# A two-layer transformer block on one core: a round's MLP parts dealt out anew over its steps, and a later start of GpSimd on the second layer's weights

## The reference

```python
def layer0(x, t):                    # 16 heads of 32, 4 key/value heads, sparse mask
    scale, shift = split(t @ W_ada.T + b_ada)
    h = layernorm(x) * (1 + scale) + shift
    q = rope(h @ Wq.T); c = h @ Wkd.T          # latent of 128
    k = rope(c @ Wku.T); v = c @ Wvu.T
    p = softmax(mask(q @ k.T / sqrt(32)))      # window 64, every 64th key, no future block
    return x + (p @ v) @ Wo.T

def layer1(x, pos, t):               # 8 heads of 64, one key/value head, no mask
    h = rms(x) * ln1_w * (1 + t @ ln1_tw.T)
    q, k, v = rope(h @ Wq.T), rope(h @ Wk.T), h @ Wv.T
    x = x + (softmax(q @ k.T / 8) @ v) @ Wo.T
    h = rms(x) * ln2_w * (1 + t @ ln2_tw.T)
    return x + (silu(h @ Wg.T) * (h @ Wu.T)) @ Wd.T    # inner width 2048
```

## Time and profile before

| | us |
|---|---|
| median of three runs | 1840.02 |
| lowest and highest | 1840.02, 1841.26 |
| the profiled execution | 1837.08 |
| its span, first to last instruction | 1835.2 |
| first pair's attention, alone | about 206.7 |
| first round | 214.0 |
| six rounds that follow, together | 1281.3 |
| last pair's MLP, alone | 133.2 |

### The profile page before, as it was taken

The page is one execution under the profiler, slowest core; times in us unless marked ns, Lnnn a source line. Parts: engine busy times, 40 slices in busy tenths (PEclk is TensorE's granted clock), DMA queues, the critical chain, the costliest instruction groups (busy, mean ns, idle before and its releaser), DMA issues.

```text
span 1835.2 us, 38092 instructions
## 1 busy us (share of the span) xinstructions
PE 1716.1 (94%) x12416; PEld 931.6 (51%) x12416; DVE 1161.6 (63%) x2956; ACT 945.7 (52%) x2775; POOL 400.3 (22%) x554
## 2 busy tenths in 40 slices
PE   6576898999999999999999999999999999999999
PEld 2244444555455545555455554555455554555444
DVE  6869566574667558684576756675586855766320
ACT  3836456364664538554483546645385544835320
POOL 6038586011111111111110111111111111101120
PEclk9777999999999999999999999999999999999999
DMA  7876489462784439653593627844395626936220
GB/s 238 142 189 113 125 198 233 100 122 72 169 162 100 81 107 195 129 116 77 130 191 88 115 75 171 158 102 79 108 195 128 118 74 136 187 90 110 98 69 23
DMA packets 527259, 234.56 MB, mean 128 GB/s; under 512 B 476336, under 2 KB 493744, under 8 KB 527024
## 3 DMA queue, kind: packets, MB, share of 16 engines
q1 hardware_dynamic: 527024, 231.72, 57.8%
HBM read 90.09 MB, written 16.78 MB: 58 GB/s over the span
## 4 chain that ended last, share of the span: by engine, by line
PE 74%; DVE 9%; DMA 9%; ACT 3%; issue 3%; SPq 1%; POOL 0%; DVEq 0%; ACTq 0%; POOLq 0%
PE up L1390 8%; PE gate L1390 8%; PE gate L1392 8%; PE gate L1391 8%; PE up L1392 7%; PE up L1391 7%; DMA prob_t<-prob 7%; PE bank L1390 4%; PE bank L1392 4%; PE bank L1391 4%; PE y L1390 4%; PE y L1392 4%; PE y L1391 4%; PE bank L1417 2%; DVE prob L1081 2%
## 5 line engine op out<-in xcount | busy, mean ns | idle before, releaser
L851 ACT ACTIVATE bank<-bank,low 128x128 f32<-128x128 f32 (+2 forms) x768 | 302.0, 394 | 74.5 <-DVE low L1074 46.8
L695 POOL TENSOR_TENSOR inner_t<-inner,inner_t 128x512 f16<-128x512 f32 x128 | 148.8, 1162 | 671.8 <-ACT inner_t L1019 671.8
L1081 DVE TENSOR_TENSOR prob<-bank,prob 128x512 f16<-128x512 f32 (+1 forms) x320 | 202.7, 634 | 47.1 <-ACT prob L860 45.7
L860 ACT ACTIVATE prob<-bank 128x512 f16<-128x512 f32 (+1 forms) x320 | 178.4, 557 | 56.2 <-DMA prob_t<-prob 33.6
L1345 DVE SCALAR_TENSOR_TENSOR silu<-silu,gate 128x512 f32<-128x512 f32 x128 | 87.9, 686 | 187.1 <-ACT silu L1013 186.0
L1390 PE MATMUL up<-mlp,ring 128*128 128x512 f16 x512 | 195.1, 381 | 5.7 <-DVE inner L1355 5.6
L1390 PE MATMUL gate<-mlp,ring 128*128 128x512 f16 x512 | 194.4, 380 | 0.9 <-DVE mlp L1050 0.9
L1391 PE MATMUL up<-mlp,ring 128*128 128x512 f16 x512 | 195.1, 381 | 0.0
L1392 PE MATMUL up<-mlp,ring 128*128 128x512 f16 x512 | 195.0, 381 | 0.0
L1392 PE MATMUL gate<-mlp,ring 128*128 128x512 f16 x512 | 194.5, 380 | 0.0
L1391 PE MATMUL gate<-mlp,ring 128*128 128x512 f16 x512 | 194.5, 380 | 0.0
(11 more groups left out here) (176 smaller groups left out, 4034.7 us busy)
## 6 DMA issues: line engine op xcount, KB each, us to landing
ring<-wgu_dram SPq DMA_DIRECT2D x112, 512.0 KB, 4.0
x_in<-x_dram SPq DMA_DIRECT2D x18, 512.0 KB, 5.0
x_res<-x_mid SPq DMA_DIRECT2D x16, 512.0 KB, 3.5
wgu_dram<-ring SPq DMA_DIRECT2D x16, 512.0 KB, 3.5
out_dram<-x_res SPq DMA_DIRECT2D x32, 256.0 KB, 2.3
prob_t<-prob SPq DMA_TRANSPOSE x256, 3.5
inner_t<-wd_t_dram SPq DMA_DIRECT2D x4, 1024.0 KB, 8.7
ring<-wg_t_dram SPq DMA_DIRECT2D x16, 256.0 KB, 3.8
```

The source lines that it names most:

```text
L695: pool.tensor_tensor(inner_t[:, 1, f, :], inner[:], inner_t[:, 0, f, :], ALU.subtract).then_inc(inner_low, 1)
L851: ins = act.activation(bank_[:, at:at + wid], bank_[:, at:at + wid], ACT.Exp, bias=low[:, j % BANKS, k:k + 1], scale=-1.0, accum_out=total)
L860: act.activation(terms(prob[:, g % SLOTS, 0, :], layer, j), terms(work_bank[USE[f"unit{layer}", j] % BANKS][:], layer, j), ACT.Copy).then_ ...
L1081: dve.tensor_tensor(terms(prob[:, slot, 1, :], layer, j), terms(work_bank[USE[name] % BANKS][:], layer, j), terms(prob[:, slot, 0, :], lay ...
```

## The change

First, `PLAN` is dealt out anew: the number of parts stays 96, 94 of them before `end`, and only their places change. By how many parts PE is ahead of the old list, step by step: none up to `unit0_7` (but for shifts of one part between neighbours among `keys` and `stack`, where PE has nothing of its own between them), one after `unit0_8`, three after `unit0_9`, two from `unit0_10` to `unit0_15`, four after `unit0_18`, four from `unit0_23` to the end of layer 0, three from `fill2.1`, two from `keys1.1`, one from `unit1_1` on, none at `unit1_5` and `unit1_6`, one from `unit1_7`, none at `unit1_12`, two after `unit1_15`, none from `out1b.0`. So four parts move from layer 1 (and the steps just ahead of it) into layer 0's units 8 to 23 and `heads0.0`.

Second, POOL waits before the first split of `wq1` until `stack_low` has reached 6, that is until all stacks of layer 0 of the first pair are made. It is one wait in the first pair; no round has it.

```diff
 PLAN = [("fill0.0", 0), ("fill0.1", 4), ("lat.0", 3), ("lat.1", 1), ("kv.0", 2), ("kv.1", 1),
-        ("query0.0", 0), ("query0.1", 0), ("keys.0", 3), ("keys.1", 0), ("query1.0", 3),
-        ("query1.1", 0), ("stack0.0", 3), ("stack0.1", 3), ("stack1.0", 3), ("stack1.1", 0),
+        ("query0.0", 0), ("query0.1", 0), ("keys.0", 2), ("keys.1", 1), ("query1.0", 3),
+        ("query1.1", 0), ("stack0.0", 2), ("stack0.1", 3), ("stack1.0", 4), ("stack1.1", 0),
...
-        ("unit0_4", 3), ("unit0_5", 1), ("unit0_6", 2), ("unit0_7", 1), ("unit0_8", 0),
-        ("unit0_9", 0), ("unit0_10", 2), ("unit0_11", 2), ("unit0_12", 1), ("unit0_13", 2),
-        ("unit0_14", 0), ("unit0_15", 2), ("unit0_16", 2), ("unit0_17", 0), ("unit0_18", 1),
-        ("unit0_19", 1), ("unit0_20", 3), ("unit0_21", 0), ("unit0_22", 2), ("unit0_23", 0),
-        ("out0a.0", 1), ("out0a.1", 0), ("heads0.0", 0), ("heads0.1", 1), ("out0b.0", 0),
-        ("out0b.1", 0), ("fill2.0", 2), ("fill2.1", 1), ("kv1.0", 1), ("kv1.1", 0),
+        ("unit0_4", 3), ("unit0_5", 1), ("unit0_6", 2), ("unit0_7", 1), ("unit0_8", 1),
+        ("unit0_9", 2), ("unit0_10", 1), ("unit0_11", 2), ("unit0_12", 1), ("unit0_13", 2),
+        ("unit0_14", 0), ("unit0_15", 2), ("unit0_16", 1), ("unit0_17", 2), ("unit0_18", 2),
+        ("unit0_19", 0), ("unit0_20", 2), ("unit0_21", 0), ("unit0_22", 3), ("unit0_23", 1),
+        ("out0a.0", 0), ("out0a.1", 0), ("heads0.0", 1), ("heads0.1", 1), ("out0b.0", 0),
+        ("out0b.1", 0), ("fill2.0", 2), ("fill2.1", 0), ("kv1.0", 1), ("kv1.1", 0),
-        ("query2.0", 0), ("query2.1", 0), ("keys1.0", 0), ("keys1.1", 1), ("query3.0", 0),
+        ("query2.0", 0), ("query2.1", 0), ("keys1.0", 0), ("keys1.1", 0), ("query3.0", 0),
         ("query3.1", 0), ("stack2.0", 1), ("stack2.1", 0), ("stack3.0", 2), ("stack3.1", 0),
-        ("scores1", 0), ("unit1_0", 1), ("unit1_1", 3), ("unit1_2", 1), ("unit1_3", 1),
-        ("unit1_4", 1), ("unit1_5", 1), ("unit1_6", 0), ("unit1_7", 2), ("unit1_8", 1),
-        ("unit1_9", 0), ("unit1_10", 2), ("unit1_11", 1), ("unit1_12", 1), ("unit1_13", 0),
-        ("unit1_14", 1), ("unit1_15", 0), ("out1a.0", 0), ("out1a.1", 1), ("heads1.0", 1),
-        ("heads1.1", 1), ("out1b.0", 1), ("out1b.1", 0), ("fill4.0", 2), ("fill4.1", 1)]
+        ("scores1", 0), ("unit1_0", 1), ("unit1_1", 2), ("unit1_2", 1), ("unit1_3", 1),
+        ("unit1_4", 1), ("unit1_5", 0), ("unit1_6", 0), ("unit1_7", 3), ("unit1_8", 1),
+        ("unit1_9", 0), ("unit1_10", 2), ("unit1_11", 1), ("unit1_12", 0), ("unit1_13", 1),
+        ("unit1_14", 1), ("unit1_15", 1), ("out1a.0", 0), ("out1a.1", 0), ("heads1.0", 1),
+        ("heads1.1", 1), ("out1b.0", 0), ("out1b.1", 0), ("fill4.0", 2), ("fill4.1", 1)]
@@ big_split_(key)
                 pool.wait_ge(*landed[key])
+                if key == "wq1":
+                    pool.wait_ge(stack_low, 3 * PAIR)
                 for src, hi in big_views(key, 0):
```

## The result

The changed kernel takes 1815.81 us, the median of four runs (1814.41 to 1817.16), beside 1840.34 for the kernel before in the same session. The ratio is 0.9866, with a 95% interval of 0.9849 to 0.9883: 24.5 us less, between 21.5 and 27.8. The forecast was 1813.5. The profiled execution has a span of 1812.6 us (before 1835.2), 22.6 less. Lines from `big_split_` on have moved down by two: L1425 is L1427, L1390 is L1392, L1260 is L1262.

A forecast was written before the change was run, and what follows sets the result against it. PE was taken to bound the six alike rounds through its stops; -18.0 (rounds), -5.0 (first round) and -3.5 (first pair) make -26.5 us, from the median 1840.02 to 1813.5, chance 0.57, range 1803 to 1833.

The forecast's parts named there:

- Which stops, and what fills them in the rounds: Layer 0's units 8 to `heads0.0`: four added parts, 5.20 us a round, fill PE stops worth 3.8, bounds 1.5 and 3.8.
- The 0.18 us that I added to each stop: After a PE stop two 193-column matmuls take 0.34 us, not 0.16; over some five stops 0.9 us a round.
- Lost cover, 0.8 us a round: Parts taken from `fill2.1` and layer 1 leave new PE stops: 0.3 plus 0.5 us a round, bounds 0 and 1.3.
- the stop expected before `fill2.1`'s second transposition: At `fill2.1` PE would wait for DVE's normalisations: a stop of 0.23 us, with the start 0.3.
- the shifts after `unit1_7`: Late in layer 1, two parts held until `out1a` end level; taken at nothing, PE's own work covering them.
- The first round: Units 8 to 23 and after: 5.0 us less, bounds 1 (transfers just as late) and 10 (idle filled, clock regained).
- The first pair: GpSimd's later start frees DVE's two-input operations before the first scores: 3.5 of 4.6 us gained, bounds 0 and 4.6.
- my deduction for SP's transpositions: First pair: not all 4.6 us come forward, since SP's six key transpositions take 7.85 us; 3.5 taken.
- the same loss at the new place, 1817.0: Moved splits slow as much two-input DVE work as before, the first pair's 3.5 us goes, sum 1817.0.
- Half comes back (1822): Stops reappear in layer 1, one DMA wait stays: rounds gain 2 us instead of 3; 1822, chance 0.25.
- Slower, as layer 1's chain stays behind: Layer 1's DVE chain doesn't come forward, 5.20 us turn into stops, 1.4 us more a round; 1846.3, chance 0.10.
- PE isn't the bound: Matmuls are held by weight loads or operands, so filling stops gains nothing; only the first pair gains: 1836.5, chance 0.08.

The follow-up runs named there:

- l1_layer1: Kernel before with four parts taken from `fill2.1` and layer 1 and done at the end of the round, layer 0 as in the old list; 1844.13 us, ratio 1.0024.
- p1_plan_only: Kernel before with the new list of parts alone, GpSimd starting as before; 1821.65 us, ratio 0.9905.
- r1_heads_back: Changed kernel with the part at `heads0.0` put back to `fill2.1`; 1821.94 us, ratio 0.9905 to the kernel before.
- g1_gaps: Changed kernel with one part moved from `unit1_13` to `unit1_12` and one from `unit0_22` to `unit0_21`; 1814.2 us, ratio 0.9858 to the kernel before.
- w1_wait_only: Kernel before, old list of parts, with GpSimd's later start alone; 1836.36 us, ratio 0.9986.
- h2_heads: Kernel before, old list, with one part moved from `heads0.1` to `heads0.0` and every chunk's end kept at its step; 1840.67 us, ratio 1.0002.
- d1_stores: Changed kernel with each store of a split chunk done twice in the first round; 1823.86 us, ratio 0.991 to the kernel before.
- u1_unit8: Kernel before with three parts given to `unit0_8` and `unit0_9`, taken back at `unit0_10`, `unit0_16` and `unit0_20`; 1842.24 us, ratio 1.0015.
- h1_heads: Kernel before, old list, with one part moved from `fill2.1` to `heads0.0`; 1856.38 us, ratio 1.0089.
- u2_unit8: Kernel before with three parts given to `unit0_8` and `unit0_9`, taken from `unit0_10`, `fill2.1` and `keys1.1`; 1854.63 us, ratio 1.0077.
- s1_stack: Changed kernel with one part, the end of chunk 5's gate product, moved from `stack0.1` to `stack1.0`; 1835.95 us, ratio 0.9976 to the kernel before.
- s2_stack: Changed kernel with two parts, the end of chunk 5's up product, moved from `stack1.0` to `stack0.1`; 1841.89 us, ratio 1.0009 to the kernel before.

## Why the prediction was right, and where it wasn't

- **Which stops, and what fills them in the rounds.** Forecast: all of 3.8 us a round, the stretch 1.4 longer, idle time under 0.7 a round. Measured: 3.5, 1.70 and 0.2. The waits of the earlier trace rows went as said. The 0.18 us that I added to each stop beyond its idle time was about right by a wrong reading: two matmuls of 193 columns show 0.33 us without a stop too (at 930.90, and the next instruction starts 0.17 later). By starts, the stop of 1.08 at `heads0.0` cost 974.14 - 972.89 less the usual 0.03, so 1.22, 0.14 more than its idle time.
- **Lost cover, 0.8 us a round.** The rounds show 16.26 / 6 = 2.71 less, so 3.50 - 2.71 = 0.8 was lost (a remainder; the two new rows are 6.0 us in six rounds), and `l1_layer1` alone costs 0.6 (0.3 to 1.0). The size was right, the places half: the stop expected before `fill2.1`'s second transposition stands at `kv1`, one step on (0.35 from one matmul's start to the next, beyond the usual 0.22), and "no wait over 0.5 for `prob`" was wrong: 1.1 at `unit1_12`. Of DVE's waits for PE in the earlier trace rows one of 1.30 remains and the 1.85 has become 0.49, so the chain did come forward. I had taken the shifts after `unit1_7` at nothing, and that is where the larger loss is.
- **The first round.** Forecast 5.0, measured 1.65. The term was mis-sized: of 8.2 us of stops in units 8 to 23 all but 2.2 went, and one of 5 came behind a transfer of 6.65 us. In four kernels with the new list and no new stop (the changed one, `p1_plan_only`, `r1_heads_back`, `g1_gaps`) the first round takes 223.4 in the mean, in four that keep the old one in the units (before, `w1_wait_only`, `l1_layer1`, `h2_heads`) 227.0; by those the term is 3.6. The reason that I gave for the low bound, transfers late because the DMA engines are full, isn't borne out: in `d1_stores` 14% more bytes a second went through with no later landings. That transfers hold PE there is right; why one of them takes over 6 us stays open.
- **The first pair.** Forecast 3.5, measured 4.75 in the one trace, 4.1 over fourteen; `w1_wait_only`, timed, leaves it at 0.4 to 5.0. The durations went to the values forecast (683, 412), nearly all of DVE's 4.6 us came forward, and my deduction for SP's transpositions was not needed. The Trainium skill, "SBUF — State Buffer", section "Who interferes with whom", has a DVE instruction with two SBUF inputs contend with a GpSimd instruction that reads SBUF; the rows agree (1066 to 684 ns), and what I made of it against the change (the same loss at the new place, 1817.0) didn't come: in 46:66, beside the moved splits, DVE's 128x512 operation with one input in PSUM (L1083) takes 687 ns, and of those with two SBUF inputs only one is there, at 692 ns.
- **The sum.** Its misses cancel in part: the first pair gave 1.25 us more than forecast, the first round 3.35 and the six rounds 1.74 less. That 1813.5 was met within 2.3 us is owed to that too, and the traces of the parts differ by 1 to 2 us between executions.
- **Half comes back (1822):** in its mechanism half right. Stops did reappear in layer 1 (1.0 us a round), but the waits for transfers went, and the rounds gave 2.71 and not 2. In the first round the 3 us of this rival were nearer to the 1.65 than my 5.0.
- **Slower, as layer 1's chain stays behind:** refuted by `l1_layer1`, 4.4 us instead of 36.
- **PE isn't the bound:** refuted by `p1_plan_only`, 17.5 us less with weight loads at the same 54% of the rounds. The Trainium skill, "Perfetto Trace Analysis", section "Identifying the Most-Contended Engine", would judge TensorE's headroom by that share and by its share of peak work; here the former hardly differs between kernels 24 us apart (684.34 of 1279.61, 681.89 of 1263.35), and the stops told what was to be had.
- **Right with a thinner reason than I knew.** I treated a stop as filled if enough parts stand ahead of it. `u1_unit8`, `h2_heads` and `g1_gaps` put parts ahead of stops that my sum would have counted, and gained nothing; `h1_heads` and `u2_unit8` lost 16 and 14 us against the kernel before, `s1_stack` and `s2_stack` 20 and 26 against the changed one. What made the change good, as I read these runs together, is that the parts ahead come from another stretch and are not taken back before the last transfer and the heads, and that the chunk ends fall where no engine that is waited for stands behind them. The first alone isn't enough: `u2_unit8` brought two parts from layer 1 and still lost 14 us. For the last there are `s1_stack` and `s2_stack`, where PE's order stays and only the place of a product's end for the other engines moves. My expectations for single moves were wrong in seven of eight cases, mostly by one omission: I priced a part by PE's time, and not by what its end sets off on the others.

## What to carry to other kernels

To fill a stop of the bounding engine, bring work from a stretch in which the others can come forward; here, work moved by a step or two within the same stretch only carried the stop along. Before such a part is moved, list for each other queue what its end places there (the product's reader, the high and low halves, the next weight load) and who stands behind that, and ask which single bank it holds. Elementwise work with two SBUF inputs on the critical chain and GpSimd's splits belong in different stretches.

## What the runs showed of the hardware that was not expected

- After some stops of 2 us and more PE goes on at its lower clock, and after others of the same length it doesn't. In `s2_stack`, after the stop of 4.39 us and one row of scores:

```profile
693.90:699.60 5.70, 5.67 (x17) 2.32 (x18) 2.69 (x17) 2.58 (x10) 0.00 (x0) 0.50 1.17 173
```

  The granted clock is 0.50 (1.2 GHz), and some 12 matmuls come 0.43 us apart instead of 0.217: 2.6 us beside the stop itself. Over the six rounds of `s2_stack`, with stops of 3.06 to 4.58 us, 7 to 13 matmuls follow so in five and none in one (3.06); of six equal stops of 2.96 in `s1_stack` four have such a tail, of six equal ones of 2.22 in `h1_heads` two. None of the stops of 1.46 us in the changed kernel's six rounds has one. So the length of a stop alone doesn't tell what it costs.
- Transfers of probabilities land in 3.0 us at the least and 3.4 in the middle, 6.6 at the most, over the changed kernel's trace. All eight of its 256 that took over 5.5 us had a load or store of the ring (256 or 512 KB) under way with them; of the 118 that had none the longest took 5.4. Most that had one weren't slow either: the middle with a ring load beside them is 3.7.
- A DMA share of 1.07 left room for 14% more bytes a second at the same place of the program (215 to 245 GB/s).
